# A two-layer scan and expert kernel: first conv block by single images, down products in groups of two pairs, other splits of gate weights and low parts, written-out orders

## The reference

```python
# conv block: z is x normalised over its 64 channels
feat = z @ in_w + in_b
inp, og, fg = jnp.split(feat, 3, axis=-1)
inp, og, lam = silu(inp), sigmoid(og), sigmoid(fg)
inp_o = einsum('...hd,...he->...hde', 1.0 - lam, inp)   # 32 heads, 2 x 2: 128 channels
s_h = scan_both_ways(inp_o, lam, axis=0)                 # h_t = lam_t * h_{t-1} + inp_t, forward + reverse
s_w = scan_both_ways(inp_o, lam, axis=1)
out = einsum('...hde,...hd->...he', s_h + s_w, og)
x = x + (layernorm(out) * gamma + beta) @ out_w + out_b

# feed-forward block: t is x normalised again, every expert is computed for every token
# layer 0: 16 experts, hidden 128:  (silu(t @ w1[e]) * (t @ w2[e])) @ w3[e]
# layer 1:  8 experts, hidden 256:  gelu(t @ W1[e] + b1[e]) @ W2[e] + b2[e]
# each weighted by the softmax over the two best gate logits (0 for the others), summed, added to x
```

## Time and profile before

| | us |
|---|---|
| median of three runs | 274.17 (271.37 to 275.12) |
| profiled execution | 270.85 |
| its span, first to last instruction | 268.9 |
| PE busy | 221.9 (83%) |
| DVE busy | 211.9 (79%) |
| ACT busy | 159.5 (59%) |
| POOL busy | 117.7 (44%) |
| mean granted TensorE clock | 0.96 of full |

### The profile page before, as it was taken

How to read it: one execution, slowest core, us unless ns; L and a number is a source line. 1 busy time by engine, 2 the same in 40 slices (tenths; PEclk the granted TensorE clock), 3 DMA queues, 4 the chain that set the end, 5 groups by cost and what they waited for, 6 DMA issues and landing times. The chain is left out here.

```text
span 268.9 us, 3812 instructions
## 1 busy us (share of the span) xinstructions
PE 221.9 (83%) x966; PEld 127.5 (47%) x966; DVE 211.9 (79%) x607; ACT 159.5 (59%) x298; POOL 117.7 (44%) x179
## 2 busy tenths in 40 slices
PE   0844268976988987899997999598599989999993
PEld 0633157634635554555562653165275454465541
DVE  5498989986999799999799999989975886342135
ACT  2552937464833665238695299129978975947550
POOL 5051992263816431267442646357335307413111
PEclk9999959999999999799998899989989999999999
DMA  1399307193049100490009500000700420410701
GB/s 35 85 197 194 75 0 157 44 211 66 0 94 201 24 1 2 109 203 6 1 7 210 102 0 1 0 4 4 156 4 0 110 49 4 123 36 22 158 20 39
DMA packets 18545, 18.52 MB, mean 69 GB/s; under 512 B 5350, under 2 KB 12284, under 8 KB 18524
## 3 DMA queue, kind: packets, MB, share of 16 engines
q1 hardware_dynamic: 18524, 18.28, 32.7%
HBM read 17.56 MB, written 0.72 MB: 68 GB/s over the span
## 5 line engine op out<-in xcount | busy, mean ns | idle before, releaser
L1209 PE MATMUL SPARE<-tok_z,up_hi 128*128 128x512 f32 x192 | 86.0, 448 | 4.6 <-DVE hidden L1114 2.9
L1210 PE MATMUL SPARE<-tok_z,up_lo 128*128 128x512 f32 x192 | 78.4, 408 | 0.0
L553 POOL TENSOR_TENSOR total<-total,weighted 128x512 f32<-128x512 f32 x39 | 50.3, 1290 | 59.0 <-DVE weighted L1135 36.5
L1322 PE MATMUL SPARE<-hidden,down 128*64 128x512 f32 x256 | 67.3, 628 | 1.5 <-DVE hidden L1114 0.9
L832 ACT ACTIVATE silu_h<-SPARE 128x512 f32<-128x512 f32 x64 | 37.1, 593 | 42.4 <-PE SPARE L1210 37.5
L1209 PEld LDWEIGHTS SPARE<-tok_z,up_hi 128*128 128x128 f32 x192 | 37.7, 197 | 51.1 <-issue 24.4
L1114 DVE TENSOR_TENSOR hidden<-silu_h,SPARE 128x512 f32<-128x512 f32 x64 | 42.5, 677 | 6.0 <-PE SPARE L1322 2.9
L1210 PEld LDWEIGHTS SPARE<-tok_z,up_lo 128*128 128x128 f32 x192 | 37.9, 197 | 5.4
L838 ACT ACTIVATE hidden<-SPARE,expert_bias 128x512 f32<-128x512 f32 x32 | 21.8, 681 | 14.4 <-PE SPARE L1210 12.6
L1322 PEld LDWEIGHTS SPARE<-hidden,down 128*64 128x64 f32 x256 | 14.4, 137 | 27.1 <-issue 17.9
L845 ACT ACTIVATE hidden<-SPARE,expert_bias 128x512 f32<-128x512 f32 x32 | 21.8, 680 | 2.1 <-PE SPARE L1210 2.1
(11 more groups left out here) (130 smaller groups left out, 365.4 us busy)
## 6 DMA issues: line engine op xcount, KB each, us to landing
gates_b<-gates_dram SPq DMA_DIRECT2D x6, 1024.0 KB, 10.0
gates_b<-gates_dram SPq DMA_DIRECT2D x8, 512.0 KB, 5.9
up_raw<-in_L_ffn_w_dram SPq DMA_DIRECT2D x4, 384.0 KB, 7.6
gates_b<-gates_dram SPq DMA_DIRECT2D x2, 768.0 KB, 10.7
up_raw<-in_L_ffn_W_dram SPq DMA_DIRECT2D x2, 512.0 KB, 6.2
up_raw<-in_L_ffn_w_dram SPq DMA_DIRECT2D x4, 128.0 KB, 3.8
down<-in_L_ffn_w_dram SPq DMA_DIRECT2D x1, 512.0 KB, 10.2
down<-in_L_ffn_W_dram SPq DMA_DIRECT2D x1, 512.0 KB, 5.0
```

The lines of the kernel that those rows point to most:

```text
L553: nc_engine.tensor_tensor(t, t, weighted[:, q % WEIGHED_RING, :], ALU.add).then_inc(s_sum, 1)
L1209: nc.tensor.matmul(dst, hi, z, start=True, stop=False)
L1210: return nc.tensor.matmul(dst, lo, z, start=False, stop=True)
L1322: last = nc.tensor.matmul(spare("down", q)[k * D:(k + 1) * D, :], w, hidden[:, at, :], start=(j == 0), stop=(j == chunks - 1))
```

## The change

Five things change together.

1. The conv block and its neighbours run by chunks. `CHUNKS` has nine: unit 0 is two chunks of one image (256 tokens), every other unit is one chunk of 512. Stages of the conv block, `e_stats`, `e_turn` and `e_z` are numbered by chunk now: chunk c is unit c - 1 from 2 on.
2. `NORM_BY_SCALAR` names chunks 2 to 8 for both kinds (before: units 3 to 7 and 2 to 7), and for these the low part is made by POOL (`low_parts`) where DVE made it.
3. In layer 0 `down` works on two pairs at a time (`DOWN_GROUP`), eight products in a row into two banks.
4. The gate weights are split once into an fp32r high and low part by DVE (`gate_w`), the logits are four products of both parts side by side, and `top` adds the two halves. The picks are read as integers without a copy, and `pick` is part of `top`. `b_res` is one instruction per tile that scales and adds, in place of a product and an addition over all tiles.
5. The simulation is gone: `ORDER` and `BANK_USES` are written-out tables.

```diff
-NORM_BY_SCALAR = {"a": (3, 4, 5, 6, 7), "e": (2, 3, 4, 5, 6, 7)}
+CHUNKS = ((0, 0, 1), (0, 1, 1)) + tuple((u, 0, GB) for u in range(1, UNITS))
+NORM_BY_SCALAR = {"a": (2, 3, 4, 5, 6, 7, 8), "e": (2, 3, 4, 5, 6, 7, 8)}
...
-DOWN_BANKS = 2
+DOWN_GROUP = (2, 1)
...
+ORDER = {
...
+    "DVE": (
+        "gate_w0 a_stats0 a_stats1 in_w0 a_parts0 b_wide0 v_wide0 b_cols0 a_parts1 add_w0 a_stats2 a_stats3 "
...
+            def low_parts(n, c):
+                k, t = c % 2, slice(0, chunk_tiles(c))
+                pool.wait_ge(s_high[n], by_scalar_up_to(n, c))
+                if c >= 2:
+                    pool.wait_ge(s_turn[n], c - 1)
+                nc.gpsimd.tensor_tensor(parts[n][:, k, t, 1, :], norm[n][:, k, t, :], parts[n][:, k, t, 0, :],
+                                        ALU.subtract).then_inc(s_low[n], 1)
...
+            def gate_weights():
+                high, low = gate_parts[:, :, 0, :], gate_parts[:, :, 1, :]
+                for l in range(LAYERS):
+                    dve.wait_ge(s_small[l], 16 * 3)
+                    e = EXPERTS[l]
+                    last = nc.vector.tensor_copy(high[:, l, 0:e], gate_raw[:, l, 0:e])
+                link(last)
+                for l in range(LAYERS):
+                    e = EXPERTS[l]
+                    last = nc.vector.tensor_tensor(low[:, l, 0:e], gate_raw[:, l, 0:e], high[:, l, 0:e].bitcast(fp32),
+                                                   ALU.subtract)
+                last.then_inc(s_gate_w, 1)
...
-                link(nc.vector.tensor_tensor(conv_y[:, :, :], heads_of(u)[1],
-                                             rstd["b"][:, u % 2, :].unsqueeze(2).broadcast_to([P, TILES, D]), ALU.mult))
-                dve.wait_ge(s_biased, u + 1)
-                r = group_rows(u)
-                nc.vector.tensor_tensor(r, r, by_tile(conv_y[:, :, :]), ALU.add).then_inc(s_conv, 1)
+                for t in range(chunk_tiles(c)):
+                    part = r[:, t // HALF, t % HALF, :]
+                    last = nc.vector.scalar_tensor_tensor(part, y[:, t, :], rstd["b"][:, c % 2, t:t + 1], part,
+                                                          ALU.mult, ALU.add)
+                last.then_inc(s_conv, 1)
...
-                link(nc.vector.tensor_copy(best_atf[:, :, :], best_at[:, :, 0:2]))
...
-                    z = tok_z[:, u % 2, t * P:(t + 1) * P].bitcast(fp32)
-                    last = nc.tensor.matmul(spare("logits", u)[:, t * e:(t + 1) * e], z, gate_raw[:, l, 0:e],
-                                            start=True, stop=True)
+                    last = nc.tensor.matmul(
+                        spare("logits", u)[:, t * 2 * e:(t + 1) * 2 * e].rearrange("p (k e) -> p k e", k=2),
+                        tok_z[:, u % 2, t * P:(t + 1) * P], gate_parts[:, l, :, 0:e], start=True, stop=True)
...
+            def down(first):
+                u = PAIR_UNIT[first]
+                l = layer(u)
+                for q in range(first, first + DOWN_GROUP[l]):
+                    wait_bank(pe, "down", q)
+                    wait_hidden(pe, 2 * q + 1)
...
+                for q in range(first, first + DOWN_GROUP[l]):
+                    i = q - pairs_before(u)
```

789 lines of the change are left out of this document (332 added, 457 removed), and 87 rows, old and new, of tables (BANK_USES, ORDER).

## The result

The changed kernel took **254.57 us** (median of 4 runs, 254.14 to 255.79) against 272.77 (269.29 to 275.12) for the kernel before on the same chip: ratio 0.9424, 95% interval 0.9341 to 0.9508. On another chip, later, it took 255.65 (6 runs) against 273.97, ratio 0.9329 (0.9291 to 0.9368). By the medians it is 18 us faster, by the two ratios 16 and 18. The ratios leave out every run that is over 1.5% above the fastest of its kernel; the medians keep all runs. The forecast was 265.5 with a range from 258: the sign was right, the size too small by 10.9, and the time lies outside the range.

The account below looks back on a forecast made before the run. DVE was taken to bound up to 178, PE after 216; 176 + 74.3 + 6 + 3.2 = 259.5, plus 1 for the clock: span 260.5, time 262.5, times 1.012 gives 265.5 us, range 258 to 277.

Parts of the forecast that it names:

- The opening: Before the first up product: DVE's head waits for gate weights, moments 8.2 us later, first up product at 54 instead of 36.99.
- The first layer: From first up product to last first-layer hid: DVE bounds, 112 us work plus 10 idle, last hid at 176.
- the down grouping: First-layer down groups on PE: 0.28 us a group, 16 groups go, 4.5 in all; only idle time while DVE bounds.
- The low parts: Subtractions of seven chunks of each kind move from DVE to POOL: 9.0 us off DVE.
- The residual: Conv residual on DVE: four tile instructions at 0.55 us replace 0.42 + 0.66; 2.6 off by the last first-layer hid.
- The late start is just earned back: At the last first-layer hid: 176, a microsecond before the old 177.0, despite the first up product at 54.
- The second layer: After the last first-layer hid: PE work 74.3 us, PE idle 6, then 3.2 to the end of the span.
- The scaling: Whole kernel: profiled time 262.5 us times 1.012, the old median 274.17 against its profiled 270.85, gives 265.5.
- A: Rival, after PE's first up product: PE's idle 21.2 us stays as latencies between engines; time 277.5, slower; chance 0.17.
- B: Rival, opening: images overlap better, first up product at 47 to 48; span 254, time 259; chance 0.13.
- C: Rival: POOL's low parts stop DVE, 10.2 of the 12.6 us saved come back; time 275.5; chance 0.2.
- the rule against part 2: DVE's savings: a POOL instruction excludes two-SBUF-input DVE instructions throughout, so 14 more on POOL could each stop DVE.

Follow-up runs that it names:

- the three with one (12.5, 3.1, 3.6): Changed kernel (255.65 us beside them) with low parts, residual, logits and down put back together: 268.15; low parts alone back on DVE: 258.79; residual alone: 259.21.

## Why the prediction was wrong in size

**The opening: right.** The gate weights landed at 8.68 and 10.66 (10.6 forecast), DVE's moments came at 11.03 (11.2), `add_w0` at 18.26 (18.3), `biases0` at 31.25 (32.3) after a wait for PE. The first up product came at 51.1 instead of 54, inside the bounds of 47 to 58: 1.0 of the 2.9 came from `biases0`, 1.9 from work between them that was sized too long. The clock stretch that I had set at 1 us at the end lies before the first up product and cost nothing extra behind it.

**The first layer: right in length, wrong in the reason.** 176 was forecast for the last `hid`, 174.5 came. DVE's 112.3 of work and 10 of idle are 114.05 and 10 in the windows. But the prediction said that a microsecond off DVE counts up to 178 and that PE's work there is only idle time on PE. That step failed, in the kernel before already: 4.1 on DVE cost 0.5 to 1.7 there and not 4, and 13.6 on PE cost 2.9 to 4.7 and not nothing. Two engines both 90% busy, each waiting for the other in turn, are not one bound and one cover; "DVE is the fuller" doesn't decide between 92 and 89%. In consequence the down grouping was worth 3.2 to 4.5 (forecast as overhead of 4.5, but thought to be hidden while DVE bounds). The low parts were worth 3.1 to 4.0. The prediction took 9.0 off DVE for them; put back they add 5.0 to its busy time, since the 0.77 that it used as the length of one was a mean of eight, three of which (1.27 to 1.37) had met POOL. The residual was worth 3.6 where its term was 2.6, within its bounds, but with two sizes wrong that cancel: four tile operations take 0.85 and not 0.55, and the pair in their place 1.41 and not 1.08.

**"The late start is just earned back": right as a balance.** The gate wait costs 5.0 at the end; other savings pay for it.

**The second layer: the step that carried the largest part of the miss.** From the last `hid` to the end 84.5 were forecast (74.3 of PE work, 6 idle, 3.2, and 1 for the clock), and 79.4 came. PE was busy 40.11 + 32.37 = 72.5 from 175, and 73.0 from 174.5, 1.3 less than the 74.3. The 81.7 from which I had subtracted contained a stretch at half clock (from 194.0, above, PE busy 2.74, of which up to 1.4 is owed to the clock), and I carried it over as work. Idle time of PE came to 79.4 - 73.0 - 3.2 = 3.2 instead of 6, and of the 2.8 most is PE's waits for `parts_e`: 3.4 in two behind the last `hid` before, 0.9 in two after. With the low parts back on DVE it is 1.2 in two, and the idle time is 3.2 as well, so in the new order it hardly matters for these waits which engine makes the low parts. I had kept the 6 because "it starts at x_res3, which the new order does not reach earlier". And the granted clock stayed at 1.00 from 51.1 to PE's last transpose, so the 1 is off too. 1.3 + 2.8 + 1.0 = 5.1; with the 1.5 at the last `hid` the span is 6.6 short of the forecast. (The windows that the sum is made of end at 178, a microsecond behind the last start of `hid`; by them the split is nearer 0.5 and 6.1.) The logits' share was taken too large: 4.4 for 1.7 to 3.0.

**The scaling: 4.3 of the miss of 10.9.** I multiplied by 1.012, because the one profiled execution lay 1.2% under the median before. The profiled execution after lay 1.2 us above its median (255.79 against 254.57): factor 3.1, and 1.2 for that. With a fourth run the median before is 272.77, only 0.7% above that execution. The kernel before varies by 2% from run to run (269.29 to 275.12) and the changed one by 0.6%, so its spread was no factor to carry over. Why it varies more is not shown.

**The rivals.** A (PE's idle time stays at 21.2) fell: it is 13.8, and PE's work behind the first up product is 185.8 where A had 193.8. It was right on one point, that PE's work counts. B (cheaper opening, 259) named the right direction; with the first up product at 51 it explains 2.9. C and **the rule against part 2**: 14 subtractions on POOL at 0.73 each did not stop DVE by anything like their 10.2, since putting them back on DVE costs 3.1 to 4.0. But the reading of the Trainium skill ("SBUF — State Buffer", "SBUF: two separate sides") that operations with two SBUF inputs are exposed does show in the residual: the addition with both inputs in SBUF takes 0.42 alone and up to 1.28 when it starts inside a POOL instruction, and the tile form, which reads one input from PSUM, never took more than 285 ns. The trace agrees with the rule in that, and I had read the gain of the tile form as instruction lengths only.

**What stays open.** How the 5.8 (or nearly 11 without the gate wait) divides between single images, normalisations on ACT and the order was not taken apart. Medians and ratios differ by up to 2.4 us for the undoings that had no changed kernel beside them; the three with one (12.5, 3.1, 3.6) are the firm numbers.

## What to carry to other kernels

Where two engines are both near 90% busy over a stretch, count a saving on either, in part, and look at what each waits for by name. Behind the first up product TensorE waited 9.6 us for the low parts of a normalisation; the new order left 3.8 of them even with the subtractions on VectorE. When you test with added work, read from the trace how much you added: one product meant as 0.23 us took 0.85. An operation placed at the head of an engine's list for a DMA that nobody needs yet can cost most of its wait at the end (5.0 of 8.0 here); put it directly ahead of its first reader. Before subtracting work from an engine's busy time, take out what that time owes to a lowered clock and don't scale by the spread of one kernel's runs.

## What the runs showed of the hardware that was not expected

In the opening of the changed kernel the 128x512 passes of the projections stand 0.43 apart from 31 to 47, with a granted clock of 1.00, and 0.43 apart from 47 to 50 at 0.57; from 51 on the same form stands 0.23 apart at 1.00:

```profile
31.00:47.00 16.00, 10.72 (x38) 8.22 (x38) 15.06 (x50) 13.96 (x26) 13.68 (x22) 1.00 0.00 1
47.00:51.00 4.00, 3.56 (x10) 2.38 (x10) 3.83 (x20) 3.92 (x8) 3.15 (x5) 0.57 0.02 4
```

```profile
32.16 0.63 PE L1232 MATMUL SPARE<-conv_z,in_hi 128*128 128x512 f32 x1
32.59 0.63 PE L1233 MATMUL SPARE<-conv_z,in_lo 128*128 128x512 f32 x1
...
52.56 0.40 PE L1232 MATMUL SPARE<-tok_z,up_hi 128*128 128x512 f32 x1
52.79 0.39 PE L1233 MATMUL SPARE<-tok_z,up_lo 128*128 128x512 f32 x1
```

So the granted clock of a window does not say at which pace the engine works in a sparse stretch; the distance between passes does.

An addition of DVE with both inputs in SBUF (128x256) that starts inside an addition or subtraction of POOL ends 0.28 us after it, in all ten such cases of the two kernels above (six with the residual in two operations, four in the kernel before); alone it takes 0.42. The form with one input in PSUM keeps 0.275 in either case (258 to 285 ns).

The two down products of a pair write different halves of the output's partitions, and their passes start within 0.06 us of each other. A second pair in a group adds 0.86 (1.87 against 1.01), and one product alone adds 0.82 to 0.85, as much as two.
